# Ordering the front of an early-fusion block: column strips, row-wise text tables, interleaved step-size units

## The chip, the cores and the metric

The kernel runs on one core of a Trainium2 chip. The metric is the device time of one execution in microseconds; of several runs the median counts. An execution has five engines with an instruction list each: TensorE (PE, with weight loads as PEld), VectorE (DVE), ScalarE (ACT), GpSimd (POOL) and SyncE (SP), which here only starts transfers. They meet through semaphores.

## The reference

Images and text become one sequence, which passes a gated state-space layer and a layer of four experts.

```python
h = _L0_tok_ref(x, W_proj, b_proj, pos_emb)              # 32 images, 36 patches of 768 values -> 256
h = concatenate([h, _L0_txt_ref(x_txt, weights)], axis=1) # 32 text places: a row of a table by position
h = h + _L0_attn_ref(_layernorm(h), ...)
h = h + _L0_ffn_ref(_layernorm(h), ...)
```

The text place looks up row `pos` of a table, where `pos` depends on the tokens and takes 34 values at most. In `_L0_attn_ref`, with 512 hidden channels and 16 states:

```python
u = x @ W_x.T + b_x ;  g = sigmoid(x @ W_g.T + b_g)
h = conv over the sequence, 3 taps per channel, of u, + conv_b
u = u * g + h * (1 - g)
dt = softplus(x @ W_dt.T + b_dt).mean(axis=(0, 1))        # one step size per channel
dt = clip(dt, 0.001, 2.0)
A_d = exp(A * dt) ;  B_d = (A_d - 1) / (A + 1e-6) * B_ssm
y = scan of u by A_d, B_d, C_ssm                          # y_t sums over earlier times
out = layernorm(x + y @ W_out.T + b_out)
```

The step size is a mean over all 32 x 68 places: no kernel of the scan can be formed before the last place is projected.

## The kernel before

Places are ordered by position, then by batch: 2176 columns are 17 tiles of 128, nine of images (`NTI`, each four patches) and eight of text (`NH0`). Channels are four chunks of 128 (`HC`). Products that need more accuracy than fp32r run as three products of high and low parts (`split3`, L490 to L494): each copy out of a bank is a high part by ScalarE and a low part by VectorE.

The front is written out by hand. `A_STEPS` (L316) is a list of steps that TensorE, ScalarE and VectorE all walk through in the same order. The steps `ring` use four banks in turn (`bank[q % 4]`); a step waits until the one four before it was read (`a_read`). They are:

- `pos` (L835): positions spread over columns; VectorE compares them with the row number and so gets the one-hot table `OH` (L1555);
- `vec` (L830): vectors and state matrices transposed; `wp` (L842): patch weights transposed, behind two `warm` products (L814);
- `tab` (L848): the 34 normalised table rows `tabx` transposed, the count of each row over all places, and sixteen small products for the mean and deviation of each text tile (L858);
- `img` (L880): three transposes of pixels `XI` of one batch half `g`, one strip of patches `wp` and one half of the 768 values, each behind one `warm` product; there are 24, batch half by batch half;
- `w` (L875): 4 transposes of one half of one weight matrix; `pt` (L860): a weight matrix times the 34 table rows, in four chunks of channels with 34 columns, 24 products each; `tt` (L867): two of these tables turned back to rows.

Every third `img` is followed by a text tile `a1` (L888), two products with `OH`. After all 24 images come the nine image tiles. Tile m goes through `a1` (18 products and two for the position, L902 to L908), `a2` (statistics on VectorE), `a3` (root on ScalarE, reciprocal and normalising on VectorE) and `a4` (two transposes, copies to `xT_hi`, `xT_lo`), one step k apart (L325). `BESIDE` (L321) puts weights and tables beside them, the first four step-size units at k = 9 and 10.

`DT_STEPS` (L405) follows: twelve units (`project_dt`, L797), a chunk of channels by a third of the image columns each, 6 products of 384 columns. A unit then goes through an exponential on ScalarE (L1277), a cap on GpSimd (L707), a logarithm on ScalarE (L1262) and a maximum with sum on VectorE (L1669). Between them stand `Gt` (the gate's table, its sigmoid by exponential and reciprocal) and the text places of chunks 0 and 1 (`T`, L953 on TensorE, `mix_text` L1624 on VectorE: gate, difference and u by `OH` from three tables).

`C_STEPS` (L413): `u` and `g` are projections of a chunk by a third, `dtr` (L981) spreads the step sizes over states, VectorE (three chunks) and GpSimd (one) form exponents times times (`powers_of`, L527), ScalarE their exponentials `Eb` (L1307). `kT` (L1016) sums over states with the weights `wsel`: 128 products with `Eb` as the weights of the array and eight columns streamed. The result `kt` goes to DRAM and comes back as Toeplitz tiles `Tb` (L603), with which the products `ssm` (L1004) apply the scan. `convolve` (L1607) and `seam` mix image places on VectorE; `uT` (L1022) turns a chunk so that time is the contraction. The list behind the first `ssm` and everything after it, the output projection, routing and experts, is ordered by a table of due times.

SyncE's queue starts tokens, vectors, the table, twelve image strips (L554), weights, then at each `H0_OUT` (L559) a store of finished tiles `h0s` to DRAM, then eight fills of zeros (L585), 11 MB in all, then the kernel's store and the Toeplitz loads. `h0s` has eight places, so tile 8 of the images is copied only when the first store of image tiles has landed (L1218).

## Time and profile before

| | |
|---|---|
| median of 3 runs | 541.32 us (535.79 to 547.62) |
| profiled execution, its own time | 537.81 us |
| its span, first to last instruction | 535.1 us |
| PE busy | 472.5 us (88%) |
| PE weight load busy | 390.6 us (73%) |
| DVE, ACT, POOL busy | 297.8, 272.6, 168.4 us |
| mean granted clock of TensorE | 0.886 |
| share of PE in the chain that ended last | 72% |

The span is what the trace shows; the execution's own time is 2.7 us longer. "Busy" adds up durations; matmuls overlap in the array, so the cadence between starts says more than one duration. The granted clock is a share of 2.4 GHz: 0.50 is the 1.2 GHz level, a mean in between is time at both.

### The profile page before, as it was taken

Reading aid. Unit: us, or ns where it says so; the run is one execution under the profiler, and the core shown is the slowest. Engines: PE = TensorE matmul, PEld = TensorE weight load, DVE = VectorE, ACT = ScalarE, POOL = GpSimd, SP = SyncE. Lnnn points to the kernel's source line nnn. Section 1 sums busy time; section 2 is a strip of 40 time slices with the busy share of each in tenths; the row PEclk is TensorE's granted clock in tenths of the full one; section 3 lists DMA queues with packets and bytes.
Section 4 is the critical chain, followed back from the end, with each engine's and each line's share of the span. In section 5 each row is a group of like instructions: output and inputs, shape, how many; then the busy total and the mean of one; then the engine's idle time right before and its main releaser. Section 6 shows DMA issues by size and latency. Waiting matters only on the chain.

```text
span 535.1 us, 10106 instructions
## 1 busy us (share of the span) xinstructions
PE 472.5 (88%) x3243; PEld 390.6 (73%) x3243; DVE 297.8 (56%) x940; ACT 272.6 (51%) x623; POOL 168.4 (31%) x268
## 2 busy tenths in 40 slices
PE   7799999849898899999999989899999999999600
PEld 5677899837698677777967766688888888888400
DVE  6433252555618642322377777786775566766574
ACT  0144231354554353452455545388587878778441
POOL 2000000053300000000124288886577855454312
PEclk8655797967877899998999999999999999999955
DMA  6940300499006444587071022223233242243162
GB/s 151 194 117 0 109 31 29 135 325 321 22 1 157 105 106 107 142 215 221 2 230 39 29 99 100 71 89 91 70 109 103 67 134 95 87 130 93 69 206 78
DMA packets 57486, 59.95 MB, mean 112 GB/s; under 512 B 23928, under 2 KB 50012, under 8 KB 56156
## 3 DMA queue, kind: packets, MB, share of 16 engines
q1 hardware_dynamic: 52988, 48.71, 34.2%
q0 software_dynamic: 3552, 9.74, 4.8%
q10 hardware_dynamic: 896, 0.87, 0.6%
q8 instruction: 27, 0.44, 0.4%
q14 instruction: 23, 0.19, 0.1%
HBM read 34.51 MB, written 24.80 MB: 111 GB/s over the span
## 4 chain that ended last, share of the span: by engine, by line
PE 72%; DVE 9%; issue 7%; POOL 4%; ACT 3%; DMA 2%; SPq 0%; DVEq 0%; POOLq 0%; ACTq 0%
PE bank L1167 13%; PE bank L492 8%; PE bank L1004 8%; PE bank L493 8%; PE bank L494 8%; PE bank L1082 3%; PE bank L814 3%; PE bank L1157 3%; POOL sorted_x L744 2%; PE bank L1021 2%; PE bank L885 2%; PE bank L1027 2%; PE bank L1139 2%; PE bank L950 1%; DMA got<-expert_y 1%
## 5 line engine op out<-in xcount | busy, mean ns | idle before, releaser
L1167 PE MATMUL bank<-w,hr 128*128 x320 | 76.0, 380 | 1.6 <-DVE ysb L1912 1.6
L1167 PEld LDWEIGHTS bank<-w,hr 128*128 128x128 f32 x320 | 60.1, 190 | 11.8 <-issue 2.8
L1403 ACT ACTIVATE hr<-bank,gsel 128x128 f32<-128x128 f32 x160 | 59.9, 460 | 0.2 <-PE bank L1157 0.2
L792 POOL DMA_INDIRECT expert_y<-ysb,toid x40 | 42.9, 1073 | 51.2 <-DVE ysb L1912 37.8
L707 POOL TENSOR_SCALAR spt<-spt 128x384 f32<-128x384 f32 x12 | 14.0, 1180 | 118.1 <-ACT spt L1277 118.1
L1004 PE MATMUL bank<-Tb,U 68*32 68x68 f32 x1024 | 47.9, 364 | 1.3 <-issue 1.3
L1004 PEld LDWEIGHTS bank<-Tb,U 68*32 68x32 f32 x1024 | 40.1, 140 | 6.3 <-issue 5.7
L1897 DVE BATCH_NORM_STATS2 bsth<-bank 128x6 f32<-128x512 f32 x40 | 27.7, 693 | 20.6 <-PE bank L494 20.1
L744 POOL DMA_INDIRECT sorted_x<-x2s,slot x34 | 33.9, 996 | 15.3 <-issue 9.2
L1395 ACT ACTIVATE hn<-bank,nmrh,rsh 128x512 f32<-128x512 f32 x40 | 31.1, 778 | 10.0 <-DVE nmrh L1906 8.1
L717 POOL MEMSET ones<- 2x128 f32 x1 | 0.2, 207 | 111.5 <-PE bank L1042 111.5
L492 PE MATMUL bank<-w_hi,bT_hi 128*128 x80 | 35.0, 438 | 0.2 <-issue 0.2
L1082 PE MATMUL bank<-Wo,yT 128*128 128x256 f32 x136 | 33.3, 387 | 1.0 <-ACT yT L1180 0.7
L494 PE MATMUL bank<-w_hi,bT_lo 128*128 x80 | 31.6, 395 | 0.0
L493 PE MATMUL bank<-w_lo,bT_hi 128*128 x80 | 31.5, 394 | 0.0
L1912 DVE COPY ysb<-bank 128x256 f32<-128x256 f32 x40 | 16.9, 422 | 25.8 <-PE bank L1167 25.2
L814 PE MATMUL bank<-busy 128*128 128x512 f32 x46 | 28.6, 698 | 1.4 <-POOL busy L657 1.4
L1082 PEld LDWEIGHTS bank<-Wo,yT 128*128 128x128 f32 x136 | 24.8, 190 | 5.7 <-ACT yT L1180 2.4
L1180 ACT ACTIVATE y<-bank 128x272 f32<-128x272 f32 x24 | 9.6, 399 | 31.9 <-PE bank L1004 31.9
L1180 ACT ACTIVATE bT_hi<-bank 128x256 fp32r<-128x256 f32 x40 | 15.3, 383 | 19.4 <-PE bank L1139 19.2
L1157 PE MATMUL bank<-ident,hn 128*128 128x128 f32 x160 | 24.1, 273 | 0.3 <-ACT hn L1395 0.3
L1566 DVE TENSOR_TENSOR pT_lo<-bank,pT_hi 128x288 fp32r<-128x288 f32 x24 | 11.0, 458 | 19.2 <-ACT pT_hi L1180 19.1
(402 smaller groups left out, 1166.1 us busy)
## 6 DMA issues: line engine op xcount, KB each, us to landing
Tb<-ssm_kernels SPq DMA_DIRECT2D x16, 680.0 KB, 4.9
sorted_x<-zpad SPq DMA_DIRECT2D x6, 1419.0 KB, 14.0
xg<-sorted_x SPq DMA_DIRECT2D x40, 129.0 KB, 2.1
got<-expert_y SPq DMA_DIRECT2D x17, 256.0 KB, 3.6
XI<-in_x_dram SPq DMA_DIRECT2D x12, 288.0 KB, 5.6
h0r<-h_spill SPq DMA_DIRECT2D x17, 128.0 KB, 2.1
out_dram<-acc SPq DMA_DIRECT2D x17, 128.0 KB
w1raw<-in_L_ffn_w_dram SPq DMA_DIRECT2D x4, 512.0 KB, 7.7
```

Source lines behind the costliest of these rows:

```text
L492: pe.matmul(out_ap, a_hi, b_hi, start=start, stop=False)
L493: pe.matmul(out_ap, a_hi, b_lo, start=False, stop=False)
L494: return pe.matmul(out_ap, a_lo, b_hi, start=False, stop=stop)
L744: pool.indirect_dma_start(xsd[p], bass.IndirectOffsetOnAxis(ap=slot[:, i, n:n + 1], axis=0), x2s[:, i, :], None).then_inc(sem("scattered") ...
L792: pool.indirect_dma_start(yd, bass.IndirectOffsetOnAxis(ap=toid[:, i % 8:i % 8 + 1], axis=0), ysb[:, i % 2, :], None).then_inc(sem(f"y_sto ...
L814: pe.matmul(ps[:], busy[:, 0:P], busy[:], start=True, stop=True)
L1004: mm = pe.matmul(bank[2 + v % 2][quad * B:(quad + 1) * B, k * L:(k + 1) * L], U2[:, j % 2, HC * h + quad, :], Tb[TOEP[q]][0:L, :, h % QH * ...
L1082: pe.matmul(ps, yT[:, i % 2, j, :], Wo[:, j, :], start=(j == 0), stop=False)
L1157: mm = pe.transpose(bank[3 + i % 2][:, c * P:(c + 1) * P], hn[:, i % 2, c * P:(c + 1) * P], ident[:])
L1167: mm = pe.matmul(bank[6][:, 0:D], hr[:, i % 3, c, :], w2[:, bass.ds(expert[i], 1), c, :].rearrange("p o n -> p (o n)"), start=(c == 0), st ...
L1395: act.activation(hn[:, i % 2, :], bank[1 + i % 2][:], ACT.Identity, scale=rsh[:, i % 2:i % 2 + 1], bias=nmrh[:, i % 2:i % 2 + 1]).then_inc ...
L1403: last = act.activation(hr[:, i % 3, c, :], bank[3 + i % 2][:, c * P:(c + 1) * P], ACT.Relu, scale=gsel[:, i, 0, c:c + 1], bias=gsel[:, i, ...
```

## The change

**Loads.** Images go first in SyncE's queue, strip by strip for both batch halves. Tokens and the table go on ScalarE's queue. Seven broadcast loads of rows are new (`cw3`, `bxr`, `cbr`, `bdg`), after the last image has been transposed. Two of the eight zero fills stand before the first store of image tiles.

**Order.** Tiles are taken as 0, 3, 6, 1, 4, 7, 2, 5, 8. The first three need patch columns 0 to 3 only, so they start after 16 of the 24 images; the other eight images stand beside them, without `warm` products. Text tiles stand behind each of the last eight of those 16. `tab` has two transposes left and stands at k = 3.

```python
IMG_ORDER = [a * TRIPLES + b for b in range(TRIPLES) for a in range(NTI // TRIPLES)]
IMAGES = [("ring", "img", half, g, wp) for wp in range(HP) for g in range(2) for half in range(2)]
EARLY = 4 * (HP - 2)
for n in range(EARLY):
    A_STEPS.append(IMAGES[n])
    if n >= EARLY - NH0:
        A_STEPS.append(("h0t", n - (EARLY - NH0)))
BESIDE = {0: IMAGES[EARLY:EARLY + 2], 1: IMAGES[EARLY + 2:EARLY + 4], 2: IMAGES[EARLY + 4:],
          3: [("ring", "tab"), ("ring", "w", 0, 0), ("ring", "w", 0, 1)],
          4: [("ring", "w", 1, 0), ("ring", "w", 1, 1)],
          5: [("ring", "w", 2, 0), ("ring", "w", 2, 1), ("ring", "vec")],
          6: [("ring", "dt", 0), ("ring", "dt", 1)],
          7: [("ln", 0), ("ln", 1), ("ring", "dt", 2), ("ring", "dt", 3)],
          8: [("ln", 2), ("ln", 3), ("ring", "pt", 0), ("ring", "pt", 2), ("a_exp",)],
          9: [("z1",), ("ring", "pt", 1), ("ring", "dt", 4), ("ring", "dt", 5)],
          10: [("ln", 4), ("ln", 5), ("z2",), ("ring", "dt", 6), ("ring", "dt", 7), ("state",)],
          11: [("ln", 6), ("ln", 7), ("ring", "tm"), ("ring", "dt", 8), ("ring", "dt", 9), ("ln", 8), ("ring", "dt", 10),
               ("ln", 9), ("ring", "dt", 11), ("ln", 10), ("ln", 11)]}
```

In a step k the parts a4, a3, a2, a1 of the tiles come first, then `BESIDE[k]`. `DT_STEPS` is gone. A unit `dt` takes one of each triple of tiles; its `ln` is the logarithm on ScalarE and the read on VectorE. GpSimd caps units 0 to 7, VectorE units 8 to 11.

**Text tables by rows.** The weights stream as 512 columns, with the 34 (for u 102, three copies) table rows as the weights of the array; `tt` and `Gt` are gone, softplus and gate are worked out as [34, 1024], and the count of rows comes out of the comparison that makes `OH`; one small product `tm` sums the text places' step sizes. A text tile's products are 258 columns wide, the last two giving mean and deviation.

```diff
@@ TensorE, pt
-                        for j in range(HC):
-                            for dc in range(DC):
-                                mm = split3(pe, ps[:, j * VOC:(j + 1) * VOC], WT[w][0][:, dc, j * P:(j + 1) * P],
-                                            WT[w][1][:, dc, j * P:(j + 1) * P], tx_hi[:, dc, :], tx_lo[:, dc, :],
-                                            dc == 0, dc == DC - 1)
+                        n = 3 * VOC if w == 1 else VOC
+                        for dc in range(DC):
+                            mm = split3(pe, ps[0:n, :], tx_hi[:, dc].rearrange("p g r -> p (g r)")[:, 0:n],
+                                        tx_lo[:, dc].rearrange("p g r -> p (g r)")[:, 0:n], WT[w][0][:, dc, :],
+                                        WT[w][1][:, dc, :], dc == 0, dc == DC - 1)
@@ ScalarE, z2
+                    act_signal(act.activation(both_, both_, ACT.Ln, bias=onec[0:VOC, :]), "zln")
+                    act_signal(act.activation(zt[:, 1], ez[:, 1], ACT.Exp, scale=-1.0), "gneg")
+                    copy(tG_hi[:], zt[:, 1]).then_inc(sem("act_front"), 1)
+                    act.wait_ge(sem("front"), front("dfix"))
+                    copy(tD_hi[:], dtmp[:]).then_inc(sem("act_front"), 1)
@@ VectorE, state
+                if step[0] == "state":
+                    constants()
+                    state_mix()
+                    continue
```

Roots are now a logarithm and an exponential on ScalarE (`a3`), so that one table of functions serves up to the sigmoid.

**Kernel sums in column groups.** The weights `wsel` have 32 columns, eight of them used in each of four accumulated products, and `Eb` is streamed; the result is turned by four transposes. All four `powers_of` are VectorE's.

```diff
@@ TensorE
-                if step[0] == "kT":
+                if step[0] == "K":
                     pe.wait_ge(sem("front"), front("wsel"))
                     for j in range(HC):
                         pe.wait_ge(sem("powers"), j + 1)
-                        for g in range(j * NG // HC, (j + 1) * NG // HC):
-                            mm = pe.matmul(ps[0:L, g * GH:(g + 1) * GH], Eb[:, g, :], wsel[:, g, :], start=True, stop=True)
+                        for m in range(4):
+                            for quad in range(4):
+                                g = j * NG // HC + quad * 4 + m
+                                mm = pe.matmul(ps[quad * 4 * GH:(quad + 1) * 4 * GH, j * L:(j + 1) * L], wsel[:, g // 4, m, :],
+                                               Eb[:, g, :], start=(m == 0), stop=(m == 3))
+                elif step[0] == "kT":
+                    who, n = c_read(ring - 1)
+                    pe.wait_ge(sem(f"c_read_{who}"), n)
+                    for j in range(HC):
+                        mm = pe.transpose(ps[0:L, j * P:(j + 1) * P], Kk[:, j, :], ident[:])
@@ order up to the first scan product
-        C_STEPS = ([("u", 0, 0), ("u", 0, 1), ("dtr",), ("u", 0, 2), ("u", 1, 0), ("u", 1, 1), ("g", 0, 0), ("g", 0, 1),
-                    ("kT",), ("u", 1, 2), ("g", 0, 2)] + [("g", 1, nb) for nb in range(NIB)] + turns(0)
+        C_STEPS = ([("u", 0, 0), ("u", 0, 1), ("dtr",), ("u", 0, 2), ("K",), ("kT",)] + text(0)
+                   + [("g", 0, 0), ("g", 0, 1), ("g", 0, 2), ("u", 1, 0), ("u", 1, 1), ("u", 1, 2)]
+                   + [("g", 1, 0), ("g", 1, 1)] + turns(0) + text(1) + [("g", 1, 2)]
                    + text(2) + both(2, 0) + ssm(0, 2) + both(2, 1) + ssm(2, 4) + both(2, 2) + ssm(4, 5) + turns(1) + ssm(5, SV)
```

On ScalarE the exponentials and the load of the sigmoid's table stand before the copies of `u` (0, 2), and these before the copy `Kk`.

## Rows read from the trace of the kernel before

**Rows 1.** Busy time by stage; columns: window, length, engines, PEclk, DMA share, GB/s

```profile
core 0: us, PE busy (x) PEld busy (x) DVE busy (x) ACT busy (x) POOL busy (x), PEclk, DMA share, GB/s
24.70:55.90 31.20, 30.84 (x113) 22.81 (x112) 11.46 (x28) 13.12 (x33) 0.00 (x0) 0.50 0.26 63
56.00:100.30 44.30, 44.30 (x297) 41.48 (x298) 17.40 (x54) 10.69 (x30) 0.00 (x0) 0.83 0.16 51
64.50:76.00 11.50, 11.50 (x93) 10.70 (x92) 7.53 (x20) 5.35 (x14) 0.00 (x0) 1.00 0.10 35
100.30:138.70 38.40, 27.88 (x107) 20.70 (x106) 20.82 (x66) 20.15 (x40) 14.02 (x12) 0.82 0.94 279
...
127.80:129.66 1.86, 1.86 (x11) 1.62 (x10) 1.65 (x9) 1.36 (x3) 0.20 (x1) 1.00 1.10 313
149.50:161.10 11.60, 11.56 (x129) 11.57 (x129) 0.00 (x0) 5.62 (x9) 0.00 (x0) 0.66 0.01 1
161.10:184.50 23.40, 20.46 (x89) 16.61 (x88) 18.51 (x35) 10.15 (x18) 0.00 (x0) 0.80 0.62 150
```

**Rows 2.** TensorE in order of time, table step and first images; columns: start, us

```profile
16.34 0.74 PE L846 MATMUL bank<-ident,Wpr 128*128 128x128 f32 x4
20.58 0.40 PE L853 MATMUL bank<-ident,tabx 34*128 34x34 f32 x2 [3.50 <-issue]
...
24.69 0.80 PE L814 MATMUL bank<-busy 128*128 128x512 f32 x1
...
25.67 0.78 PE L814 MATMUL bank<-busy 128*128 128x512 f32 x1
...
28.54 0.79 PE L814 MATMUL bank<-busy 128*128 128x512 f32 x1
```

**Rows 3.** TensorE in order of time, image tiles, weights, tables, step-size units

```profile
55.97 0.55 PE L492 MATMUL bank<-WpT_hi,pT_hi 128*128 128x256 f32 x1 [0.43 <-ACT h0s L1180]
...
60.80 0.47 PE L492 MATMUL bank<-WpT_hi,pT_hi 128*128 128x256 f32 x1
...
63.65 1.10 PE L879 MATMUL bank<-ident,Wr 128*128 128x128 f32 x8
...
74.88 0.28 PE L492 MATMUL bank<-tx_hi,WTdt_hi 128*128 128x34 f32 x1
...
77.58 0.43 PE L916 MATMUL bank<-ident,xs 128*128 128x128 f32 x2
...
102.68 0.42 PE L492 MATMUL bank<-xT_hi,WTdt_hi 128*128 128x384 f32 x1
...
104.87 0.38 PE L916 MATMUL bank<-ident,xs 128*128 128x128 f32 x2
```

**Rows 4.** Groups by line, step-size units on the other engines; busy, mean ns, idle

```profile
L707 POOL TENSOR_SCALAR spt<-spt 128x384 f32<-128x384 f32 x12 | 14.0, 1180 | 118.1 <-ACT spt L1277 118.1
...
L1669 DVE SCALAR_TENSOR_TENSOR spj<-bank,vec,spt 128x384 f32<-128x384 f32 x12 | 7.4, 617 | 10.9 <-ACT spt L1262 10.9
L1262 ACT ACTIVATE spt<-spt,onec 128x384 f32<-128x384 f32 x12 | 7.3, 612 | 4.2 <-POOL spt L707 4.2
```

**Rows 5.** Groups by line, powers, exponentials, table load, text mix, scan products

```profile
L531 DVE TENSOR_TENSOR Eb<-adt,kio 128x1088 f32<-128x1088 f32 x3 | 5.5, 1888 | 0.2 <-DVE adt L1692 0.2
...
L1638 DVE SCALAR_TENSOR_TENSOR hb<-bank,vec,hb 128x512 f32<-128x512 f32 x6 | 4.5, 750 | 0.2
L1307 ACT ACTIVATE Eb<-Eb 128x1088 f32<-128x1088 f32 x4 | 4.3, 1109 | 0.7 <-DVE Eb L531 0.5
...
L1308 ACT ACT_TABLE_LOAD x1 | 1.3, 1283 | 0.0
...
L1004 PE MATMUL bank<-Tb,U 68*32 68x68 f32 x1024 | 47.9, 364 | 1.3 <-issue 1.3
```

**Rows 6.** SyncE in order of time, the twelve image loads

```profile
7.21 16.61 SPq L554 DMA_DIRECT2D XI<-in_x_dram  x12
```

More of the change, by code:

```diff
@@ L293, in build_kernel @@
         state = lambda n: ins[n].rearrange("(c p) s -> p c s", p=P)
-        TILE_ORDER = list(range(NTI, NT)) + list(range(NTI))
+        TRIPLES = HP // 2
+        IMG_ORDER = [a * TRIPLES + b for b in range(TRIPLES) for a in range(NTI // TRIPLES)]
         H0_OUT = [(0, NH0), (NH0, NH0 + 3), (NH0 + 3, NH0 + 6), (NH0 + 6, NT)]
-        def ready_tiles(nb):
-            return (BLOCKS[nb][0] + BLOCKS[nb][1]) // P
-        PREP = [("pos", 0), ("pos", 1), ("vec",)] + [("wp", c) for c in range(0, CK, 2)] + [("tab",)]
@@ L307, in build_kernel @@
-        IMAGES = [("img", half, g, wp) for g in range(2) for wp in range(HP) for half in range(2)]
-        WEIGHTS = [("w", w, dc) for w in range(3) for dc in range(DC)]
-        TABLES = [("pt", 0), ("pt", 1), ("pt", 2), ("tt", "U"), ("tt", "D")]
-        A_RING = PREP + IMAGES + WEIGHTS + TABLES
-        ring_hi = lambda q: sum(1 for step in A_RING[:q + 1] if step[0] in ("wp", "img", "w"))
-        TAB = PREP.index(("tab",))
-        W0 = len(PREP) + len(IMAGES)
-        PT0 = W0 + len(WEIGHTS)
@@ L325, in build_kernel @@
         for k in range(NTI + 3):
             A_STEPS += [(f"a{s + 1}", k - s) for s in (3, 2, 1, 0) if 0 <= k - s < NTI]
[L327 removed]
+            A_STEPS += BESIDE[k]
+        A_RING = [step[1:] for step in A_STEPS if step[0] == "ring"]
+        ring_hi = lambda q: sum(1 for step in A_RING[:q + 1] if step[0] in ("wp", "img", "w"))
+        LAST_EARLY = A_RING.index(IMAGES[EARLY - 1][1:]) + 1
+        LAST_IMAGE = A_RING.index(IMAGES[-1][1:]) + 1
+        BY_POOL = 8
@@ L856, in _ @@
-                        for t in range(NH0):
-                            c0 = (DC + 1) * VOC + 2 * t
-                            mm = pe.matmul(ps[:, c0:c0 + 2], OH[0:VOC, t * P:(t + 1) * P].bitcast(F32), rnt[:],
-                                           start=True, stop=True)
+                            mm = pe.transpose(ps[:, dc * VOC:(dc + 1) * VOC], tabx[:, dc * P:(dc + 1) * P],
+                                              ident[0:VOC, 0:VOC])
                     elif kind == "pt":
@@ new lines, in _ @@
+                if step[0] == "state":
+                    act.wait_ge(sem("act_front"), act_front("a_exp"))
+                    act.activation(atmp[:], atmp[:], ACT.Ln, bias=onec[:]).then_inc(sem("act_front"), 1)
+                    continue
+                kind, m = step
+                if kind == "h0t":
+                    act.wait_ge(sem("h0_ps"), m + 1)
+                    copy(h0s[:, m, :], bank[4 + m % 2][:, 0:DX]).then_inc(sem("h0_copied"), 1)
+                    continue
+                i = IMG_ORDER[m]
@@ L1308, in _ @@
-            act.preload_act_table_set("sigmoid_and_others")
-            for step in C_STEPS:
-                if step[0] == "u":
-                    if step[1] > 0:
-                        u_parts(step[1], step[2])
+            act.wait_ge(sem("front"), front("pad1"))
+            for step in C_STEPS:
+                if step == ("u", 0, 2):
+                    act.wait_ge(sem("adt"), 1)
+                    act.activation(wmix[:], adt[:], ACT.Exp).then_inc(sem("act_front"), 1)
+                    for j in range(HC):
+                        act.wait_ge(sem("adt"), j + 2)
+                        g = slice(j * NG // HC, (j + 1) * NG // HC)
+                        act.activation(Eb[:, g, :], Eb[:, g, :], ACT.Exp).then_inc(sem("powers"), 1)
+                    act.preload_act_table_set("sigmoid_and_others")
+                if step[0] == "K":
+                    q = C_RING.index(step)
+                    act.wait_ge(sem("c_ps"), q + 1)
+                    copy(Kk[:].rearrange("p c k -> p (c k)"), bank[q % 2][:, 0:HC * L]).then_inc(sem("c_read_act"), 1)
+                elif step[0] == "u":
+                    u_parts(step[1], step[2])
@@ new lines, in _ @@
+                if step[0] == "ln":
+                    d = step[1]
+                    q = A_RING.index(("dt", d))
+                    dve.wait_ge(sem("dt_ln"), d + 1)
+                    if d >= 2:
+                        dve.wait_ge(sem("a_read"), A_RING.index(("dt", d - 2)) + 1)
+                    dve.scalar_tensor_tensor(spj[:, d % 2, :], bank[q % 4][:, 0:NI // NIB],
+                                             vec[:, bdt0 + d % HC:bdt0 + d % HC + 1], spt[:, d % 4, :], ALU.add, ALU.max,
+                                             accum_out=dts[:, d % HC, d // HC:d // HC + 1]).then_inc(sem("a_read"), 1)
+                    continue
```

640 lines of the change are left out of this document (293 added, 347 removed).

## The prediction

> **What bounds the kernel now.** I read the page first, then busy time by stage, then TensorE's order of time up to the first scan product, then the groups by line. The span is 535.1 us. The change touches only what stands ahead of the scan products (L1004), whose first one starts at 184.5; the lists and the work behind it are the same in both kernels. So the question is when that moment comes.
>
> The stages ahead of it have different limits. From 24.7 to 55.9 TensorE is busy for 30.84 of 31.20 us, at a granted clock of 0.50, the 1.2 GHz level. From 56.0 to 100.3 it is busy throughout, at 0.83 on the mean. From 100.3 to 138.7, the step sizes, it is busy for 27.88 of 38.40 us and waits for other engines. From 149.5 to 161.1 it forms the kernel sums. From 161.1 to 184.5 VectorE is busy for 18.51 of 23.4 us, and TensorE's text products stop for its reads. [rows 1]
>
> **The change, step by step.** I follow TensorE, since the order is written out for it. All times are from the start of the span.
>
> *Start of the images.* Before, the last patch-weight transposes end at 17.08, then `tab` waits 3.50 us and runs from 20.58 to 24.69 [rows 2]. After, nothing stands between, and the three `vec` transposes ahead of them are gone too (about 1 us, bounds 0 and 1). Images start at 16.5 instead of 24.7. The data is there: XI's twelve issues took 16.61 us from 7.21 [rows 6], and now stand first in SP's queue, so strip 3 is issued by about 12. The three token loads go from SP's queue to ScalarE's and share the engines with XI; I price that at 0 to 1.5 us, and take 0.
>
> *Images.* One image with its warm product takes 25.67 - 24.69 = 0.98; three of them with one text tile take 28.54 - 24.69 = 3.85, so a text tile costs 0.97 or less [rows 2]. Sixteen images and eight text tiles are 24 x 0.96 = 23.0 at this clock, where before there were 24 and eight. The first image tile starts at 39.5 (before 55.97 [rows 3]).
>
> *Nine image tiles, with what lies beside them.* At half clock a tile takes 60.80 - 55.97 = 4.83, at full clock 63.65 - 60.80 = 2.85. Eight transposes take 1.10 at most, 0.14 each; the other eight images carry no warm product and cost 3 x 0.14 = 0.41. A pair of step-size units takes 104.87 - 102.68 = 2.19, or 0.18 per 384-column product. Before, a text table (`pt`) took 77.58 - 74.88 = 2.70 in 24 products of 34 columns, three times; now it is six of 512 columns, 6 x 0.18 x 512/384 = 1.46. [rows 3] By step k:
> k0 4.83 + 0.8 = 5.6; k1 2.85 + 0.8 = 3.7; k2 2.85 + 1.6 + 1.0 = 5.5 (four images in a row on four banks, with two copies each to be waited for: 1.0, bounds 0.3 and 2); k3 2.85 + 0.27 + 1.1 + 0.3 = 4.5; k4 4.2; k5 4.6 with `vec`; k6 and k7 2.85 + 0.27 + 2.2 = 5.3 each; k8 3.1 + 2.9 = 6.0. Sum 44.7, so k8 ends at 84.2. The same 44.3 us held nine tiles and three tables before, but now four step-size units and eight images are in it. The full clock is my choice here: from 64.5 to 76 tiles with eight transposes between them ran at 1.00 [rows 1].
>
> *k9 to k11, no tiles left.* TensorE has 11 us of work; VectorE and ScalarE set the pace. The table of exponentials is now 34 x 1024, priced by the nearest row, 1.11 us for 128x1088 on ScalarE [rows 5]. In k10 ScalarE has two copies, two logarithms (0.61 each [rows 4]), the 1.1, then 0.6 each for the gate's exponential and two copies; VectorE ends its reads of them about 10.3 us behind k8. Then VectorE does `state`: six short operations for the mixing and about ten constants, at 1.86/9 = 0.2 each [rows 1], and a memset: 4.3 us. Behind it in VectorE's queue stands the last tile's low part (`a4` of tile 8), for which units 8 to 11 wait. So they begin at 84.2 + 10.3 + 4.3 + 0.4 = 99.2, after an idle stretch of TensorE, at half clock at first: 4 x 1.6 = 6.5. The last unit then passes exponential, cap, logarithm and read: 0.6 + 0.4 + 0.6 + 0.7, with 0.2 of queueing [rows 4]. All step sizes are read at 108.2; before it was 138.0. GpSimd's cap of 1.18 us per unit [rows 4] is off the path: it has a whole step k for two units, and VectorE takes the last four.
>
> *Step size to kernel sums.* Mean, spread product and exponent scale: 1.6. Four powers on VectorE at 1.89 (GpSimd no longer takes one): 7.55. Mixing weights between the first and second: 1.3. Last exponential 1.1, table load 1.28, u's two copies 1.2, the copy of the sums 0.5, four transposes 0.6. [rows 5] Sum 15.1, end at 123.3; before, it took 161.1 - 138.0 = 23.1. The old 128 products filled 11.6 us at 0.66 clock [rows 1]. The new 64 have 32 columns of the array each, like the scan products, whose 1024 were busy for 47.9 us, 0.047 each [rows 5]: 16 take 0.75, behind the last power. If they don't run side by side, 0.23 each, that is 3.7.
>
> *Kernel sums to the first scan product.* Before 23.4, but four text products were done earlier. Now: text 0 4.4 (starts at half clock), three g 3.3, then the turns wait for VectorE. Its list is the kernel copy, two text mixes (four operations of 0.7), and three convolutions with the seam: 14.3 behind the sums (18.51 us of it stood in the old stretch [rows 1], a mix at 0.75 [rows 5]). Turns 5.2, text 1 4.0, g 1.1, text 2 behind the last convolution 5.7, u and g 2.2: 32.5. The scan starts at 155.8, before at 184.5.
>
> *Loads.* SP now waits for the last image, then issues seven broadcast rows, two zero fills, and only then the first image tiles' store, for which tile 8's copy waits. By SP's old pace this lands some 5 us ahead of need; I price it at nothing, and 5 us if that cover is gone. GpSimd's work on the rows (four operations, some 6 us) has until k9.
>
> Sum: 184.5 - 155.8 = 28.7 us off. The profiled execution took 537.81 us (span 535.1), 3.5 below the median of the three runs, 541.32. So 509 against it, 512.6 against the median; I say **511**.
>
> **Rivals.**
> *A, the clock stays at 1.2 GHz.* Images are transposes, and in their stretch TensorE was busy all the time at 0.50 [rows 1]. If two images beside each tile hold it there up to the scan, the 40 us of work from k1 to k8 double (+40) and some 20 us of the later 32 come on top: 571, slower by 5%. It decides once more than 29 us of work run at half clock beyond what I count. Against it: tiles between transposes at 1.00 from 64.5 to 76, and the small products of `pt`, behind which a tile slowed, are gone. The Trainium skill (TensorE: Matmul & The Clock Gate, Part 4: PE-mode transpose) says that transposes do not count as busy for the clock in the usual way; the image stretch agrees, and by that rule alone rival A would hold where images are dense, for three of the nine tiles, which is 6 us.
> *B, the step-size chain is longer.* Each unit's four hand-overs, the broadcast rows late, or the store behind the zero fills: 10 to 15 us of the gain stay on the path, 521 to 526. For it: in the old stretch TensorE stood 10.5 of 38.4 us.
> *C, the kernel sums run one after another.* +3 to +7 us with half clock: 514 to 518. The same skill page (Part 3: Packing small matmuls) has tiles in different column groups run concurrently; with that this rival is worth nothing, and the scan products' 0.047 agree.
> *D, better.* If the clock rises during the images, 23 us become 12: 500.
> *E, nothing gained.* VectorE's total work isn't less; if half clock and late hand-overs meet, 531 to 550.
>
> **How the numbers follow.** Forecast with C, 505 to 518: 0.60. B 0.17, D 0.10, E 0.08, A 0.05. Range 499 to 526: it leaves out A, E and the ends of B and D. Faster by over 2% (about what a measurement of this kernel can tell from no change, since its three runs spread over that) in the first three: 0.87; within 2% 0.08; slower 0.05.
>
> **What would show it.** First image transpose near 16.5; first image tile near 39.5; granted clock near 1.00 from 45 to 84; nine tiles done near 81; an idle TensorE behind unit 7 that ends with VectorE's last low part, not with GpSimd; last step size read near 108; kernel sums done near 123, with the last quarter of them under 1 us; first scan product near 156; from there 350.6 us as before. I am wrong if the clock is 0.5 in the tiles, if the first image waits for XI or the tokens, if tile 8's copy waits for the store, or if the stretch behind the scan's start changes by more than 4 us.

## The result, and the profile after

| | before | predicted | after |
|---|---|---|---|
| median | 539.91 us (535.79 to 547.62, 4 runs) | 511 us (499 to 526) | 503.12 us (501.94 to 503.78, 4 runs) |
| profiled execution, its span | 537.81, 535.1 us | 509, 506.4 us | 503.78, 502.0 us |
| mean granted clock | 0.886 | | 0.920 |

After over before is 0.934, with an interval of 0.928 to 0.940. The medians count every execution, while the ratios, here and below, leave out those in which a kernel ran slower at a lower granted clock, so a ratio is not quite the quotient of two medians. The time came out inside the range, 8 us under the forecast. Landmarks in the profiled executions, in us from the start of the span:

| | before | predicted | after |
|---|---|---|---|
| first image (its warm product) | 24.69 | 16.5 | 12.38 |
| first image tile | 55.97 | 39.5 | 27.68 |
| k = 8 done (last table product `pt` of that step) | | 84.2 | 70.18 |
| step-size units 8 to 11 begin | | 99.2 | 88.82 |
| last step size read | 138.0 | 108.2 | 98.9 |
| kernel sums done (after: turned back) | 161.1 | 123.3 | 111.7 |
| first scan product | 184.5 | 155.8 | 152.0 |
| from there to the end | 350.6 | 350.6 | 350.0 |

So the change won 11.8 us more than forecast by the first image tile, and gave 7.8 of them back between the kernel sums and the scan. Busy time by stage of the kernel after, which answers [rows 1]; the columns are window, length, the five engines, granted clock, DMA share and GB/s:

```profile
core 0: us, PE busy (x) PEld busy (x) DVE busy (x) ACT busy (x) POOL busy (x), PEclk, DMA share, GB/s
12.40:27.68 15.28, 13.68 (x82) 10.07 (x81) 9.82 (x23) 10.51 (x27) 0.52 (x2) 1.00 1.15 212
27.70:66.00 38.30, 36.23 (x269) 32.96 (x269) 15.97 (x45) 14.19 (x43) 6.49 (x6) 1.00 0.54 179
66.00:82.00 16.00, 10.53 (x51) 7.57 (x52) 11.65 (x30) 11.69 (x27) 6.30 (x5) 0.94 1.06 334
83.20:88.80 5.60, 0.01 (x1) 0.01 (x1) 5.01 (x18) 1.82 (x5) 2.12 (x2) 0.50 1.06 340
88.80:99.00 10.20, 8.75 (x36) 8.45 (x36) 6.02 (x20) 5.18 (x10) 1.82 (x1) 0.76 0.12 36
103.20:111.70 8.50, 4.54 (x133) 3.38 (x133) 3.47 (x3) 6.07 (x7) 0.00 (x0) 0.70 0.01 2
111.70:152.00 40.30, 38.45 (x137) 26.73 (x136) 24.22 (x45) 15.77 (x28) 0.00 (x0) 0.71 0.35 87
```

Before, the image stretch stood at 0.50 [rows 1]. Here images and tiles run at 1.00 from 12.4 to 66. TensorE is idle from 83.2 to 88.8, and from 111.7 on the clock averages 0.71 while TensorE is busy for 38.45 of 40.3 us. Instructions of TensorE in order of time, after (start, duration, engine, line, operation, and in brackets the idle time before it with what ended it); the first five answer [rows 2], the others [rows 3]:

```profile
12.38 0.50 PE L815 MATMUL bank<-busy 128*128 128x512 f32 x1
12.71 0.41 PE L884 MATMUL bank<-ident,XI 96*128 96x96 f32 x3
...
16.47 0.48 PE L815 MATMUL bank<-busy 128*128 128x512 f32 x1
16.79 0.41 PE L884 MATMUL bank<-ident,XI 96*128 96x96 f32 x3
16.98 0.48 PE L815 MATMUL bank<-busy 128*128 128x512 f32 x1
...
27.68 0.36 PE L490 MATMUL bank<-WpT_hi,pT_hi 128*128 128x256 f32 x1 [0.72 <-DVE pT_lo L1570]
...
67.24 0.42 PE L490 MATMUL bank<-WTdt_hi,tx_hi 128*34 128x512 f32 x1 [1.25 <-DVE spj L1589]
...
71.68 0.48 PE L490 MATMUL bank<-WTx_hi,tx_hi 128*102 128x512 f32 x1 [1.24 <-DVE spj L1589]
...
81.37 1.84 PE L864 MATMUL bank<-cnt,ez 34*128 34x2 f32 x8 [2.50 <-DVE ez L1599]
88.82 0.66 PE L490 MATMUL bank<-xT_hi,WTdt_hi 128*128 128x384 f32 x1 [5.61 <-DVE xT_lo L1628]
```

An image with its warm product takes 16.98 - 16.47 = 0.51 instead of 0.98. The units 8 to 11 wait for the last tile's low part, as the prediction said. The groups by line of 60 to 112 us, which answer [rows 4, 5]:

```profile
L726 POOL TENSOR_SCALAR spt<-spt 128x384 f32<-128x384 f32 x8 | 10.1, 1281 | 10.6 <-ACT spt L1206 10.6
L1218 ACT ACTIVATE spt<-spt,onec 128x384 f32<-128x384 f32 x12 | 7.2, 612 | 8.4 <-POOL spt L726 7.3 <-DVE spt L1546 1.0
L1589 DVE SCALAR_TENSOR_TENSOR spj<-bank,vec,spt 128x384 f32<-128x384 f32 x12 | 7.2, 613 | 7.4 <-ACT spt L1218 7.2
L529 DVE TENSOR_TENSOR Eb<-adt,kio 128x1088 f32<-128x1088 f32 x4 | 5.0, 1286 | 0.1
L1305 ACT ACTIVATE Eb<-Eb 128x1088 f32<-128x1088 f32 x4 | 4.4, 1111 | 2.5 <-DVE Eb L529 2.3
```

A power takes 1.29 us; before, a mean of 1.89 stood there [rows 5].

### The profile page after: what moved, and what is told of

Read it like the earlier page. It is cut to its first block, busy times and chain, and to the rows that moved or that the text cites. A ratio compares the mean times of both kernels' runs of the same rounds, so it can differ in the third digit from the quotient of the medians.

```text
span 502.0 us, 9958 instructions
## 1 busy us (share of the span) xinstructions
PE 436.0 (87%) x3163; PEld 354.9 (71%) x3163; DVE 296.9 (59%) x927; ACT 274.4 (55%) x634; POOL 172.3 (34%) x273
## 4 chain that ended last, share of the span: by engine, by line
PE 62%; DVE 10%; issue 6%; SPq 6%; ACT 6%; DMA 4%; POOL 4%; DVEq 0%; POOLq 0%; ACTq 0%
PE bank L1157 14%; PE bank L988 9%; PE bank L490 7%; PE bank L491 6%; PE bank L492 6%; SPq L541 4%; PE bank L1072 3%; PE bank L1147 3%; DMA h_spill<-h0s 3%; PE bank L1017 3%; POOL sorted_x L759 2%; PE bank L948 2%; PE bank L1129 2%; ACT U L522 1%; PE bank L949 1%
## 5 line engine op out<-in xcount | busy, mean ns | idle before, releaser
L1157 PEld LDWEIGHTS bank<-w,hr 128*128 128x128 f32 x320 | 60.1, 190 | 11.8 <-issue 2.7
L1394 ACT ACTIVATE hn<-bank,nmrh,rsh 128x512 f32<-128x512 f32 x40 | 31.1, 777 | 10.3 <-DVE nmrh L1901 8.4
L1172 ACT ACTIVATE bT_hi<-bank 128x256 fp32r<-128x256 f32 x40 | 15.3, 383 | 18.9 <-PE bank L1129 18.6
L1637 DVE SCALAR_TENSOR_TENSOR hb<-ur,ncw,hb 128x352 f32<-128x352 f32 (+2 forms) x12 | 7.4, 616 | 26.8 <-ACT gb L1287 26.8
L753 POOL TENSOR_TENSOR h0r<-h0r,lnb_b 128x256 f32<-128x256 f32 x17 | 13.3, 787 | 24.0 <-ACT xb L1346 21.3
L1147 PEld LDWEIGHTS bank<-ident,hn 128*128 128x128 f32 x160 | 18.9, 141 | 1.2 <-ACT hn L1394 0.6
## 6 DMA issues: line engine op xcount, KB each, us to landing
sorted_x<-zpad SPq DMA_DIRECT2D x6, 1419.0 KB, 11.6
```

The lines of the kernel that those rows point to most:

```text
L1147: mm = pe.transpose(bank[3 + i % 2][:, c * P:(c + 1) * P], hn[:, i % 2, c * P:(c + 1) * P], ident[:])
L1157: mm = pe.matmul(bank[6][:, 0:D], hr[:, i % 3, c, :], w2[:, bass.ds(expert[i], 1), c, :].rearrange("p o n -> p (o n)"), start=(c == 0), st ...
L1394: act.activation(hn[:, i % 2, :], bank[1 + i % 2][:], ACT.Identity, scale=rsh[:, i % 2:i % 2 + 1], bias=nmrh[:, i % 2:i % 2 + 1]).then_inc ...
```

## The experiments

Each run has its own runs of the kernel before beside it on the same chip, with medians of 540 to 542 us. Ratios are to those.

### Where the image stretch gets its clock

**The kernel before, with the wait ahead of `tab` filled.**

```diff
                     elif kind == "img":
                         warm(ps, 1)
+                    elif kind == "tab":
+                        warm(ps, 8)
```

> The kernel before, with eight more warm products of 128x512 in front of the table step, where TensorE stood idle for 3.5 us at 17 to 20.6. Question: why did the images run at 1.2 GHz before and at 2.4 GHz after? Theory 1 (the clock fell because of idle and thin work ahead of the images, and a stream of images that is 45% streaming keeps whichever level it finds): the granted clock from 24.7 on is near 1.00, the images end some 12 us sooner, time 525 to 530. Theory 2 (images at their old density hold the clock at 1.2 GHz whatever was before them; the denser text tiles of the change raised it): clock stays 0.50, time within 1 us of before.

Measured: 537.12 us (529.5 to 549.75), ratio 0.988 (0.981 to 0.994). By stage:

```profile
16.30:20.77 4.47, 2.95 (x13) 2.26 (x11) 3.28 (x7) 0.78 (x2) 0.00 (x0) 0.88 1.36 198
20.77:24.04 3.27, 3.27 (x28) 3.11 (x29) 0.47 (x4) 0.48 (x2) 0.00 (x0) 1.00 1.36 201
24.04:53.25 29.21, 28.78 (x108) 21.25 (x106) 10.98 (x24) 12.66 (x32) 0.00 (x0) 0.50 0.28 70
```

The eight products brought the clock to 1.00. It lasted through the twenty small products of `tab` and two images, and fell to 0.50 at the third (24.04). It stayed there for the other 29 us. That is neither theory: the clock rose and was lost again. The ratio is 1.2% under one, with its interval clear of one; in the profiled execution the first image tile comes 2.7 us earlier, and where the rest comes from is not shown. Filling the wait did not carry the clock through the images.

**The kernel before, with twelve such products behind `tab`.** They stand between the small products and the first image, where the run above had eight ahead of the small products.

```diff
                     elif kind == "img":
-                        warm(ps, 1)
+                        warm(ps, 12 if A_RING[q - 1][0] == "tab" else 1)
```

> The kernel before with twelve products of 512 columns between the table step (20 small products, behind which the clock fell at the third image in the run with eight filled products) and the first image; nothing else is changed. Theory 1 (the image stretch keeps the level it starts with, one product of 512 columns for each image is enough to hold 1.00 but not to reach it): first image near 27 at clock 1.00, 24 images and eight text tiles in 15 to 18 us instead of 28 to 31, first image tile near 43 to 46 instead of 56, time 528 to 532 with before at 540. Theory 2 (the old kernel's order of images, batch half by batch half with a text tile behind every third, does not hold 1.00 whatever stands ahead): clock back at 0.50 within the first four images, first image tile near 58, time 541 to 543.

Measured: 525.67 us (525.11 to 527.0), ratio 0.975 (0.969 to 0.980), as theory 1 said and a little under its 528 to 532. By stage:

```profile
17.27:24.87 7.60, 4.11 (x20) 4.13 (x21) 2.58 (x6) 0.78 (x2) 0.00 (x0) 0.70 1.41 193
24.87:30.16 5.29, 5.29 (x14) 4.03 (x13) 0.47 (x4) 0.23 (x1) 0.00 (x0) 0.50 1.18 275
30.16:47.82 17.66, 16.94 (x112) 13.29 (x111) 10.89 (x24) 12.92 (x32) 0.00 (x0) 0.99 0.09 28
```

The twelve products ran at 0.50, and the clock rose as they ended. Then the old 24 images with their eight text tiles ran at 0.99 and took 17.7 us instead of 31.2. Nothing else in their order, loads or products differs from before. So the same run of images stood at 0.50 throughout before and at 0.99 here, and the level came from what stood ahead of it. That is the cause of the term of 23.0 us in the prediction. In the old kernel it alone is worth 11 us between the profiled executions (spans of 535.1 and 524.1) and 14 between the medians, with the 5.3 us of products paid.

Two things stay open. In the run above the clock was at 1.00 when the images began and fell all the same; ahead of them it had fewer such products, then an idle 1.5 us, then the twenty small ones, and no run parts these. And the images do not keep 1.00 in every execution. With all 24 of them first in the changed kernel (a run further down, whose profiled execution took 506.07 us, the slowest of its five) they began at 1.00, and the clock was at 0.50 from 26 us, amid images with their warm products:

```profile
24.82 0.50 PE L815 MATMUL bank<-busy 128*128 128x512 f32 x1
...
25.94 0.80 PE L815 MATMUL bank<-busy 128*128 128x512 f32 x1
```

**The changed kernel without warm products ahead of the images.**

```diff
-                    elif kind == "img" and q < LAST_EARLY:
-                        warm(ps, 1)
```

> The changed kernel without the warm product in front of each of its 16 early images; nothing of the result depends on them. If they hold the clock up: it falls to 0.50 within the images, each image costs more than the 0.2 us that its warm product took, and the first image tile starts within 2 us of 27.7 or later; tiles start at half clock (+2 us): time +1 to +4 us. If the clock holds without them: 16 x 0.2 = 3.2 us less on TensorE, but the two copies per image (0.46 on VectorE) then set the pace of 0.5 us per image: 0 to -1 us.

Measured: 507.64 us (505.0 to 509.58), ratio 0.943 (0.937 to 0.949). The image stretch:

```profile
14.79:31.55 16.76, 14.54 (x66) 10.54 (x65) 8.98 (x22) 10.27 (x27) 0.00 (x0) 0.59 0.99 214
```

The median is 4.5 us over the changed kernel's, a little more than the 1 to 4 expected, and the intervals of the ratios still meet. The clock averages 0.59: it was 1.00 at the first images and 0.50 from 18 on, although 16 products are gone. The stretch takes 16.76 us instead of 15.28. The first image tile starts at 31.55 instead of 27.68, but 2.4 of these 3.9 us were there before the first image, which came late by itself (see the last section). The Trainium skill (TensorE: Matmul & The Clock Gate, Part 4: PE-mode transpose) says that transposes do not count as busy for the clock in the usual way, and this run agrees, though TensorE also stood for 0.74 and 1.06 us shortly before the fall. What the prediction lacked was the other half: with one ordinary product beside each image the stretch ran at 1.00 in the changed kernel.

**Warm products ahead of the eight images beside the tiles, too.**

```diff
-                    elif kind == "img" and q < LAST_EARLY:
+                    elif kind == "img":
```

> The changed kernel with one product of 512 columns ahead of each of the eight images beside the tiles too. Theory 1 (the stretches of half clock at 36 to 48 in three of the profiled variants come from images without such products): clock 1.00 from 12 to 80, time 1 to 3 us under the changed kernel: 500 to 502. Rival (the fall is chance, or comes from the wait for the copies): half clock between 28 and 48 as often as before, 502 to 504.

Measured: 505.41 us (504.65 to 505.88), ratio 0.937 (0.932 to 0.941), not to be told from the changed kernel by its interval, and by the median above what either theory had. The clock was 1.00 from 12 to 64 in the profiled execution. But the changed kernel's own profiled execution had that without them. Nothing was gained. Why the clock falls between 36 and 48 us in some profiled variants stays open.

### The order of the front

**All 24 images ahead of the first tile.**

```diff
-        EARLY = 4 * (HP - 2)
+        EARLY = 4 * HP
-        BESIDE = {0: IMAGES[EARLY:EARLY + 2], 1: IMAGES[EARLY + 2:EARLY + 4], 2: IMAGES[EARLY + 4:],
+        BESIDE = {0: [], 1: [], 2: [],
```

> The changed kernel with all 24 images (each with its warm product) ahead of the first tile, the text tiles behind the last eight; no tile is begun early. Eight images at 0.51 come in front, 4.1 us, and eight at 0.2 us each plus stalls of 0.76 and 1.31 behind copies go: +1 to +2 us if beginning early matters only by that; +4 us or more if tiles and images really overlapped; 0 or less if the early begin is worth nothing.

Measured: 498.78 us (497.89 to 506.07), ratio 0.928 (0.923 to 0.932), a miss: I had expected a small loss. Four of its five executions took 497.9 to 498.8 us, under all of the changed kernel's, but the intervals of the ratios meet. So beginning three tiles early, which the change is built around, is worth nothing measurable. The eight warm products that this run adds don't explain it, since alone they gained nothing (the run with them beside the tiles). TensorE has the same work in either order, and it is the engine that sets the pace up to 66 us. In the best run below, which has this order too, the first `pt` stands at 66.20, against 67.24 in the changed kernel.

**The state's mixing and the constants at k = 7 instead of k = 10.**

```diff
-                  7: [("ln", 0), ("ln", 1), ...
+                  7: [("a_exp",), ("state",), ("ln", 0), ("ln", 1), ...
```

> The changed kernel with the constants and the state mixing (83.1 to 88.2 on VectorE) moved from k = 10 to k = 7, where VectorE stood idle for 5.5 us. Theory (units 8 to 11 wait for tile 8's low part, queued behind this block): they begin about 5 us sooner, TensorE's idle stretch of 5.6 us shrinks to under 1, time -4 to -5 us. Rival (ScalarE's list of logarithms and copies sets the moment anyway): -1 us or less.

Measured: 500.3 us (497.14 to 503.23), ratio 0.926 (0.917 to 0.934). The median is 3 us lower, but the intervals meet. In its profiled execution 36 to 48 us ran at half clock, so the first `pt` came 6.2 us later than in the changed kernel (73.45 against 67.24), and still units 8 to 11 began only 1.1 us later (89.89 against 88.82): TensorE's wait for tile 8's low part was 1.35 us instead of 5.61.

**Both together.** 

> The changed kernel with all 24 images ahead of the first tile and the constants and the state's mixing at k = 7. Theory 1 (both gains are real and in different places: no images without warm products beside the tiles, and 5 us of VectorE's work out of the stretch in which TensorE stands): units 8 to 11 begin near 85 instead of 88.8, last step size read near 95, time 495 to 498. Rival (both only move the same wait: the tables' chain pt, z1, z2 sets when tile 8's low part is written): 499 to 501.

Measured: 495.47 us (494.78 to 496.11), ratio 0.918 (0.914 to 0.923). That is clear of the changed kernel's 0.928 to 0.940. The order of time on TensorE, where units 8 to 11 begin:

```profile
80.13 1.83 PE L864 MATMUL bank<-cnt,ez 34*128 34x2 f32 x8 [2.49 <-DVE ez L1599]
83.01 0.66 PE L490 MATMUL bank<-xT_hi,WTdt_hi 128*128 128x384 f32 x1 [1.05 <-DVE xT_lo L1628]
```

The wait of 5.61 us has become 1.05. The last step size is read at 92.2, not 98.9, although the first image came 2.2 us later in this execution.

**And the tables' second part behind tile 8.** `z2` moves from k = 10 to the head of k = 11, behind `a4` of tile 8, and `tm` to the end. Two of the last logarithms also stand one unit later.

```diff
-                  10: [("ln", 4), ("ln", 5), ("z2",), ("ring", "dt", 6), ("ring", "dt", 7)],
-                  11: [("ln", 6), ("ln", 7), ("ring", "tm"), ("ring", "dt", 8), ...
+                  10: [("ln", 4), ("ln", 5), ("ring", "dt", 6), ("ring", "dt", 7)],
+                  11: [("z2",), ("ln", 6), ("ln", 7), ("ring", "dt", 8), ... ("ln", 11), ("ring", "tm")]}
```

> As the run before it, and z2 (softplus and gate of the tables) stands behind a4 of tile 8 in the lists of ScalarE and VectorE, with the small product tm behind the last unit. Theory 1 (TensorE's idle stretch from 83 to 89 in the changed kernel is only an order of VectorE's queue): units 8 to 11 begin within 2 us of unit 7, the last step size is read 3 to 5 us earlier than in the run before it, time lower by 2 to 5 us: 491 to 496. Rival (VectorE's and ScalarE's work in this stretch is the bound, so the tables' work only changes places with the units'): the units begin earlier, the last read is not, time equal within 1.5 us or later by up to 2.

Measured: 493.3 us (491.74 to 494.2), ratio 0.914 (0.908 to 0.919), all of its runs below all of the run before it. TensorE, in order of time:

```profile
78.32 0.66 PE L490 MATMUL bank<-xT_hi,WTdt_hi 128*128 128x384 f32 x1 [2.51 <-DVE xT_lo L1628]
...
86.21 1.05 PE L864 MATMUL bank<-cnt,ez 34*128 34x2 f32 x8 [0.79 <-DVE spj L1589]
```

The units begin 4.7 us earlier than in the last run, the last step size is read 3.9 us earlier (88.3), of which 1.7 were there by the first `pt` already. So 2.2 us came out of the order in the lists, with no work taken away. About 1.0 of them is a collision that the new order happens to avoid: GpSimd's fill of `wsel` now starts behind the last cap (see the last section). This is the best kernel of the study, 2% under the changed one.

### The kernel sums

**The old sums in the changed kernel**: `Eb` as weights, eight columns streamed, no copy and no turning.

```diff
-                                mm = pe.matmul(ps[quad * 4 * GH:(quad + 1) * 4 * GH, j * L:(j + 1) * L], wsel[:, g // 4, m, :],
-                                               Eb[:, g, :], start=(m == 0), stop=(m == 3))
+                            mm = pe.matmul(ps[0:L, g * GH:(g + 1) * GH], Eb[:, g, :], wsel[:, g, :], start=True, stop=True)
```

> The changed kernel with the old kernel sums: 128 products with the exponentials as weights, eight columns streamed, no copy and no four transposes behind them. Theory (the column groups are worth their share): 128 products at 0.09 are 11.6 us and begin with the first quarter of the powers, so they overlap the powers' last 5 us; end of sums some 4 to 6 us later, minus the copy, transposes and waits of 2.9 us: +2 to +4 us. Rival (the sums hide behind the powers in either form): within 1 us.

Measured: 510.18 us (507.37 to 511.25), ratio 0.948 (0.942 to 0.954), 7 us more, where 2 to 4 were expected. TensorE in order of time:

```profile
106.41 14.64 PE L1003 MATMUL bank<-wsel,Eb 128*68 128x8 f32 x128 [1.41 <-ACT Eb L1297]
```

Before, these filled 11.6 us at a clock of 0.66 [rows 1]; here 14.64 us, from 106.41 to 121.05, at 0.50. In the changed kernel the last quarter starts at 107.87 and ends at 109.01. From the last step size to the copy `kt` it is 19.1 us here and 12.8 there, a difference of 6.2, and all of it is in the time. I had expected less, because I left the half clock out.

The trace has two entries for each of these products: the code issues 64 in either form, and the profile counts 128. So the 128 products of the texts above are 64. In the changed kernel the 16 products of a quarter took 0.68 us at full clock and 1.14 in the last quarter at half, where rival C had 3.7: rival C fell. The Trainium skill (TensorE: Matmul & The Clock Gate, Part 3: Packing small matmuls) says that products in different column groups run at the same time. These times agree with it, but no run has the same products without groups.

### Loads, and the late half clock

**All zero fills behind the stores**, to take away tile 8's wait.

```diff
-                for _ in range(2):
-                    zero_rows(*zeros.pop(0))
```

> The changed kernel with all eight zero fills behind the last store of tiles, instead of two behind each store. In the changed kernel tile 8's copy stood until 70.0 for a store that was queued behind two fills, though its product was done at 66.0. Theory (this wait is on the path to the last step size): the copy comes at 66.0, units 8 to 11 some 3 to 4 us sooner, time -3 to -4 us. Rival (VectorE's and ScalarE's lists hide it, or the cap on GpSimd, late by its own wait, takes its place): -1 to 0 us. If the fills now collide with the kernel's store: up to +3 us.

Measured: 503.65 us (501.59 to 508.23), ratio 0.933 (0.925 to 0.940): no difference. In the changed kernel ScalarE waits for the store that stands behind two fills:

```profile
70.02 0.38 ACT L1172 ACTIVATE h0s<-bank 128x256 f32<-128x256 f32 x1 [0.79 <-DMA h_spill<-h0s]
```

Its tile was ready at 66.0, so the copy is 4.0 us late. That is the price the prediction named and put at nothing. Without the fills in front the copy stands without a wait. But from the first `pt` to units 8 to 11 it takes 21.2 us instead of 21.6, and TensorE's last wait there is 5.61 us as before, for the low part behind `state`. The store's lateness is covered by that wait.

**Keeping TensorE busy around the kernel sums**: ten, four (four times) and eight unused products ahead of `dtr`, each quarter of K, and `kT`.

```diff
+            def keep(count, ps=bank[6]):
+                for _ in range(count):
+                    pe.matmul(ps[:, 0:384], WT[1][0][:, 0, 0:P], xT_hi[:, 0, 0:384], start=True, stop=True)
...
+                        keep(KEEP[1])
                         pe.wait_ge(sem("powers"), j + 1)
```

> The changed kernel with products without use (128x384, 0.18 us each at full clock) in TensorE's idle time: 10 ahead of the spread product, 4 ahead of each quarter of the sums, 8 ahead of the four transposes. Theory (the half clock from 108 to 121 comes from the idle and thin work between 97 and 111): clock near 1.00 there, six text products and the first projections take 3 to 5 us less, time -2 to -4 us. Rival (the clock falls all the same, or VectorE's mixes set the pace): within 1 us, or +1 to +2 from products that come in the way.

Measured: 505.37 us (504.06 to 506.47), ratio 0.938 (0.930 to 0.945). By stage:

```profile
103.00:113.40 10.40, 9.18 (x155) 7.23 (x154) 4.97 (x9) 7.30 (x8) 0.00 (x0) 0.84 0.01 2
113.40:118.60 5.20, 4.72 (x18) 2.16 (x16) 2.67 (x6) 1.19 (x2) 0.00 (x0) 0.93 0.33 57
118.60:136.00 17.40, 16.53 (x89) 14.00 (x89) 12.78 (x24) 10.72 (x20) 0.00 (x0) 0.92 0.72 184
136.00:152.40 16.40, 15.38 (x42) 9.56 (x41) 8.76 (x16) 3.86 (x7) 0.00 (x0) 0.58 0.00 0
```

The text products of chunk 0 now take 4.7 us at 0.93 instead of 6.7 at 0.50. But the products put in delayed the sums by 2.2 us (`kt` at 113.99, not 111.74), and in text 1, behind the turning of chunk 0, the clock is at half again. The scan starts at 152.4, as before.

**Two such products ahead of each of the eight turns of chunk 0.**

> The changed kernel with two such products ahead of each turn of chunk 0 (16, 2.9 us of work, 1.2 us of it in gaps). Theory (the thin turns let the clock fall at about 139 and it stays at 0.50 until 152): clock near 1.00 from 139 to 152, 5 us of that stretch saved, net -2 to -4 us. Rival (VectorE's convolutions and mixes set the end of the stretch): +1 to +2 us.

Measured: 507.7 us (504.7 to 507.89), ratio 0.940 (0.932 to 0.948), not faster. The clock held 1.00 until 146, when TensorE ran into a wait of 2.05 us for VectorE's `hb` in text 2, and was at 0.50 by 148. The turns had grown from 5.1 to 7.0 us. In this profiled execution the front was 2.2 us late by itself, so the stretch counts: from the first turn to the scan it took 23.6 us, against 23.1 in the changed kernel. How to carry the full clock from 108 to 152 for less than it costs stays open.

## Why the prediction was right

The direction, the path and most of the waits held: the front moved ahead in the stretches named, the tail stayed (350.0 against 350.6), and rival A fell. That the total is near is partly luck. One mechanism was wrong, the clock in the images, and two large terms missed in opposite directions:

| step | predicted | measured | difference |
|---|---|---|---|
| span's start to first image | 16.5 | 12.4 | -4.1 |
| 16 images, 8 text tiles | 23.0 | 15.3 | -7.7 |
| tiles, k0 to k8 | 44.7 | 42.5 | -2.2 |
| k8 done to units 8 to 11 | 15.0 | 18.6 | +3.6 |
| units to last step size | 9.0 | 10.1 | +1.1 |
| step size to kernel sums | 15.1 | 12.8 | -2.3 |
| sums to first scan product | 32.5 | 40.3 | +7.8 |
| the rest (350.6, 350.0), and outside the span (2.7, 1.8) | 353.3 | 351.8 | -1.5 |

The sum is -5.3, which leads from 509.1 to the profiled 503.8: -17.8 in five rows and +12.5 in three. The median of 503.1 lies inside the range, but under the 505 to 518 that had the chance of 0.60. And one of the prediction's own signs of being wrong came up: tile 8's copy did wait for the store.

- **Images.** The term of 23.0 was priced at 0.50, because the old stretch stood there [rows 1]. That row showed a level and not a cause. The level came from what ran ahead, 20 small products and an idle engine, and the change takes both away. Rival D had this with 12 us for the images and a chance of 0.10; it measured 15.3. TensorE waited 1.5 us for the copies, and an image with a text tile took 1.11 us, more than half of the 1.91 before. Its 500 was nearer than the forecast's 511. The start at 12.4 has the same source in part: the patch-weight steps took 2.8 us, most of it at full clock, and 5.2 before.
- **The idle stretch** was predicted with its cause, and measured with it: 18.6 us from k8 to the units, of which TensorE stood for 2.5 and 5.6. VectorE ended its reads 12.9 us behind k8 instead of 10.3, and constants and mixing took 5.2 us instead of 4.3. The later runs show that the places of `state` and of `z2` were the price: these two waits, 8.1 us together, went down to 3.5 and then to 2.5.
- **Units to the last step size.** The 6.5 us of products came as predicted. The excess of 1.1 is VectorE's last cap, 1.37 us instead of 0.36 (see the last section).
- **The powers** were priced at 1.89 each from a group in which GpSimd worked beside VectorE [rows 5]. Alone, each takes 1.29: 5.0 us instead of 7.55. The sums themselves were priced by mixing two counts: 0.047 us is the scan's cadence per entry of the trace, two of which are one product, while 16 is a count of products in the code. By one count it would have been 1.5 us; 0.68 to 1.14 were measured.
- **From the sums to the scan** is the term that failed: 32.5 us predicted, 40.3 measured. I counted half clock for the first text products only. It held from 108 to about 121 and again from 138 to 151.6:

```profile
111.70:121.00 9.30, 9.30 (x22) 5.86 (x22) 3.83 (x7) 1.64 (x3) 0.00 (x0) 0.50 0.69 169
121.00:128.90 7.90, 7.71 (x43) 7.06 (x42) 7.31 (x15) 5.13 (x10) 0.00 (x0) 1.00 0.94 241
138.00:151.60 13.60, 13.07 (x31) 8.51 (x31) 7.24 (x13) 3.23 (x6) 0.00 (x0) 0.50 0.00 1
```

  A pair of text products takes 1.15 us there and 0.66 at full clock. In the prediction VectorE's own work set the start of the turns, 14.3 us behind the sums. They started after 17.2, for VectorE itself stood for 5.5 us, for text 0 (6.7 us instead of 4.4) and the first gate, which ran on TensorE at half clock. That is 2.9 us of the 7.8. The turns took 5.1 us, as predicted. Behind them text 1 took 0.6 more than counted, its g 1.1, text 2 with a short wait 1.6, and the last u and g 1.8. As with the images, a level was taken from one stretch and not asked for its cause. That the idle time and thin work ahead bring it down is borne out by the filled run, where text 0 ran at 0.93.
- **The image strips** (twelve issues in 20.70 us from 0.79, against 16.61 from 7.21 in [rows 6]) kept ahead of TensorE, as forecast.
- **Rival B** was half true: the broadcast rows and the store were late. The run without fills shows that the store's lateness cost nothing. For the rows no run shows it: GpSimd waited for them until 59.35 and capped the first unit at 64.6, 6.9 us after its exponential, and the first `pt` on TensorE waited 1.25 us for that unit's read.

## What to carry to other kernels

A granted clock read in one stretch isn't a property of that stretch: ask what ran ahead of it, and price both levels. A short run of wide products between small products and a dense row of transposes can be worth more than it costs (5.3 us put in, 11 to 14 us gained net here). With one wide product beside each group of transposes the level then held in nine of the ten profiled executions of the changed front that had it. Where an engine stands at the end of a front, look for the order in another engine's queue before its load: three moves in the lists gave 2% here, and one of them took the early begin of tiles back.

## What the runs showed of the hardware

**Two engines on one operation.** Before, VectorE's three powers took 5.51 us in a row, and GpSimd's one 2.01 beside them; after, three of VectorE's take 3.69. So VectorE lost 1.82 us to an operation of 2.01 on GpSimd, more than the 1.29 that the fourth power costs it alone. Both read two tiles of SBUF. Two lines of before, then one of after:

```profile
143.06 5.51 DVE L531 TENSOR_TENSOR Eb<-adt,kio 128x1088 f32<-128x1088 f32 x3 [0.23 <-DVE adt L1692]
143.00 2.01 POOL L531 TENSOR_TENSOR Eb<-adt,kio 128x1088 f32<-128x1088 f32 x1 [6.30 <-DVE adt L1692]
...
102.98 3.69 DVE L529 TENSOR_TENSOR Eb<-adt,kio 128x1088 f32<-128x1088 f32 x3
```

The Trainium skill (GPSIMD Engine Reference, 1. Specifications) names VectorE instructions with two SBUF inputs as those that contend with GpSimd, and these traces agree.

**A fill beside a cap.** After, VectorE's caps of units 8 to 10 take 0.36 us each. The last one takes 1.37, beside GpSimd's fill of `wsel`, which nothing needs at that moment:

```profile
95.17 0.36 DVE L1546 TENSOR_SCALAR spt<-spt 128x384 f32<-128x384 f32 x1 [0.39 <-ACT spt L1206]
...
96.21 1.37 DVE L1546 TENSOR_SCALAR spt<-spt 128x384 f32<-128x384 f32 x1
...
95.55 1.82 POOL L728 MEMSET wsel<- 128x2048 f32 x1 [10.23 <-PE bank L492]
```

The last logarithm waits 1.00 us for that cap, on the way to the last step size. In the best run the fill starts at 87.33, behind the last cap, and all four caps take 0.36 or less.

**Broadcast rows.** The changed kernel's loads that repeat a row over 34 or 102 partitions were slow. Busy time by stage, after:

```profile
40.20:43.20 3.00, 2.54 (x20) 2.44 (x20) 1.48 (x5) 0.20 (x1) 0.00 (x0) 1.00 0.27 98
43.20:47.50 4.30, 4.30 (x36) 3.99 (x36) 2.83 (x7) 2.44 (x8) 0.00 (x0) 1.00 0.22 78
47.50:51.40 3.90, 3.90 (x32) 3.63 (x32) 2.46 (x6) 2.21 (x7) 0.00 (x0) 1.00 0.12 52
```

A share of 0.12 is that of two of sixteen DMA engines, at 52 GB/s; the stretch with the fills, from 83.2 to 88.8, moves 340. The rows landed only at 59.35, 20 us behind their first issue. The fills are not the cause: in the run without them it was 20.9 us. The Trainium skill (DMA: Bandwidth & Descriptors, Why a DMA increments its semaphore by 16 and not by 1) says that a transfer is split over the largest number up to 16 that divides the slowest dimension of both its sides. By that a load of 34 rows gets 2 engines and one of 102 rows 6, an estimate. The share of 0.12, with the loads of 34 rows in flight, agrees with the 2; no stretch shows the others alone.

**The same instructions, other clocks.** The first transposes of an image came at 12.7 in seven of the profiled executions with the changed kernel's start, at 13.4 in one and at 14.8 or 14.9 in three others, with a clock of 0.70 or 0.71 from 12 to 16 in those. None of their edits is ahead of that moment. So a difference of 2 us between two profiled executions of a front like this one is not yet an effect of an edit.
